# A selective state-space layer beside an MLP: the decay factors in PSUM, C turned on GpSimd, and another order at the end of a sequence's VectorE program

## The chip, the cores and the metric

The kernel runs on one core of one Trainium2 chip. The metric is the device time of one launch, in microseconds (us), that is from the first instruction to the last as the device reports it. A core has five engines with a queue of instructions each: TensorE (PE in the profile; its weight loads are PEld), VectorE (DVE), ScalarE (ACT), GpSimd (POOL), and SyncE (SP), whose queue issues the DMAs here. Every engine takes its own instructions strictly in order. What has to wait for another engine waits on a semaphore, and all that stands behind it in the same queue waits too.

## What is computed

Eight sequences of 512 tokens, 128 features wide. Each is normalised, and the result is the input plus a state-space branch plus an MLP branch. Cut to what matters:

```python
xn   = layernorm(x)                                   # (8, 512, 128)
z, xBC, dt = split(xn @ in_proj_w.T)                  # 256, 256+64+64, 4 heads
dt   = softplus(dt + dt_bias)
x_ssm, B, C = split(silu(causal_conv4(xBC)))
B_c, C_c = complex(B[0::2], B[1::2]), complex(C[0::2], C[1::2])   # 32 pairs
theta = clip(theta_base + tanh(xn @ w1) @ w2, -pi/2, pi/2)        # (4 heads, 32)
log_z = complex(-(lambda_base + eta * theta**2) * dt, theta * dt)
# chunks: S_t = exp(cumlog_t) * S_0 + sum_{s<=t} exp(cumlog_t - cumlog_s) * B_s * (x_ssm*dt)_s
y    = real(C_c . S) + D * x_ssm
g    = rmsnorm(y * silu(z)) * norm_w
attn = g @ out_proj_w.T
mlp  = s2 * relu2(s1 * relu2(s0 * [xn, -xn] @ K0) @ K1) @ K2      # K of +1 and -1, 128-512-512-128
out  = x + attn + mlp
```

The decay of a pair (s, t) is split into a factor of s and a factor of t, so that a product of matrices does the sum: with phase p and summed log decay c, K = exp(-c) (cos p, sin p) on the side of s, Q = exp(c) C (cos p, sin p) on the side of t, and U = Q times B for the part that needs B at the side of t.

## The kernel before

State data is laid out as 128 partitions (4 heads of 32 pairs) by 512 tokens, so most operations of VectorE, ScalarE and GpSimd are one instruction on a tile of 128x512 numbers of 4 bytes. The eight sequences are software-pipelined by hand: each engine has a function `pipelined(n, ...)` that writes out its order for the front of sequence n (projections, phases, decays, MLP), the back of sequence n-1 (G products, states, y, gate, output projection) and the start of sequence n+1 (layernorm, its transposes, the projection of dt, x, B and C). A loop of three rounds runs two sequences each; sequences 0, 7 and the last back stand outside it. There is no scheduler: the order of the code is the order of the queues, and a class `Signal` counts the steps of each stage on a semaphore. `s_kq` counts the steps of `decayed`, `s_u` those of `u_products`, `s_dt` the small steps of dt, `s_mo` the sum of the MLP (`add_mlp`), `s_bk` those of `b_and_k`.

The pieces that the change touches, by engine:

- VectorE, `dt_input` and `dt_steps`: softplus of dt as a chain of tiny instructions on 128x16 numbers, each waiting for the one ahead. All tiles lie in SBUF.
- VectorE, `exponents`: the log decay `lz` (L580), its running sum (L586), and the sum clipped (L587), after which ScalarE takes exp(-c) into `E` and exp(c) into `E2` (`decays`).
- VectorE, `decayed`: part 0 makes Kre and Kim (L603, L604). Part 1 makes `ec`, `es` (L608, L609). Parts 2 and 3 turn C by the phase (L613 to L615, three instructions each) into Qre and Qim.
- GpSimd: `b_and_k` (B times the conjugate of K, six instructions) and then `u_products` (Q times B, six instructions, L1141 to L1144), which waits for all of `decayed`.
- TensorE: the order around the seam between two sequences is `mlp1` (L1310, L1311), `x_products(n + 1, 0)` (L1262), `mlp_out` (L1319), `bc_products(n + 1)` (L1273), `lora1` of the next sequence (L1248), then the G products of the back, L1329, which wait for `s_mo`, `s_dt` and `s_u`, and `g_across` (L1339), which waits for `s_bk`.
- VectorE's tail of a sequence: `h1_low` 2 and 3 (L723, which release `mlp_out`), `x_times_dt` (L539), `dt_steps` of the next sequence, `add_mlp` (L727), `largest` (L651).

## Time and profile before

| What | us |
|---|---|
| Median of 3 runs | 410.99 (410.89 to 411.18) |
| The profiled execution, its own time | 410.37 |
| Its span (first to last instruction) | 407.0 |
| From one sequence's first G product to the next one's, in the middle | 44.3 |

The profiled execution lies 0.6 us under the median, and 3.4 us of its time lie outside the span. A busy time of an engine is the sum of its instructions. The chain of waits is followed back from the last instruction: each step is what released the one behind it. In a timeline row a bracket tells how long the engine stood idle ahead of the instruction, and who ended that. The mean granted TensorE clock of the execution was 0.941 of full speed.

### The profile page before, as it was taken

To read this page: it belongs to the slowest core of one execution; us is meant where nothing else is said; L and a number is where in the kernel's file an instruction comes from. 1 tells how busy PE (TensorE), PEld (TensorE's weight loads), DVE (VectorE), ACT (ScalarE), POOL (GpSimd) and SP (SyncE) were. 2 spreads that over 40 slices of the span, in tenths; PEclk is the share of its full clock that TensorE was granted. 3 is DMA by queue.
4 is the path that set the end of the run, shared out by engine and by line. 5 is a ranking of instruction groups with operands and counts; after the bars stand their busy time and mean duration, and the time that the engine had idled before them with its cause. 6 is when DMAs were issued, how large, how long until landed. Compare 5 with 4: busy or idle time off the path is not lost.

```text
span 407.0 us, 9993 instructions
## 1 busy us (share of the span) xinstructions
PE 334.8 (82%) x3962; PEld 234.9 (58%) x3962; DVE 310.3 (76%) x655; ACT 171.7 (42%) x305; POOL 147.6 (36%) x124
## 2 busy tenths in 40 slices
PE   0469289889979997989979997999799997895582
PEld 0444146577657664776567765766477655752571
DVE  2695789688968897789958896889868994888221
ACT  0307643375317714473427531771447343651020
POOL 1001077107621465107810762136610880076301
PEclk9999579999989999999989998999989998998896
DMA  7101200320023001400031002300040003000001
GB/s 192 15 0 40 64 0 2 81 52 2 27 61 73 2 0 42 108 14 0 27 84 48 2 27 62 73 2 2 26 122 11 0 27 85 23 2 26 2 2 31
DMA packets 19097, 14.86 MB, mean 36 GB/s; under 512 B 5045, under 2 KB 14826, under 8 KB 19050
## 3 DMA queue, kind: packets, MB, share of 16 engines
q1 hardware_dynamic: 16090, 13.67, 12.8%
q10 hardware_dynamic: 2960, 0.49, 0.7%
q8 instruction: 37, 0.61, 0.6%
q14 instruction: 10, 0.08, 0.1%
HBM read 3.67 MB, written 2.10 MB: 14 GB/s over the span
## 4 chain that ended last, share of the span: by engine, by line
DVE 47%; PE 26%; issue 11%; ACT 10%; POOL 2%; DMA 2%; SPq 1%; DVEq 1%; ACTq 0%; POOLq 0%
PE bank L1329 6%; PE bank L1420 4%; DVE h1l L723 3%; PE bank L1397 3%; DVE tmpd L614 3%; PE bank L1281 2%; DVE xd L539 2%; DVE phl L554 2%; DVE tmpc L613 2%; PE bank L1339 2%; DVE cum L586 2%; DVE ds L521 2%; DVE dacc L525 2%; DVE osb L736 2%; ACT z L970 2%
## 5 line engine op out<-in xcount | busy, mean ns | idle before, releaser
L1310 PE MATMUL bank<-h0h,W 128*128 128x512 f16 x128 | 50.3, 393 | 4.7 <-DVE h1l L723 3.2
L1160 POOL TENSOR_TENSOR btmp<-Kre,bres 128x512 f32<-128x512 f32 x8 | 8.5, 1059 | 125.5 <-DVE Kim L604 125.5
L1311 PE MATMUL bank<-h0l,W 128*128 128x512 f16 x128 | 50.1, 392 | 0.0
L1262 PE MATMUL bank<-XW,xh 128*128 128x256 f16 x256 | 49.1, 280 | 0.0
L1113 POOL TENSOR_TENSOR rstd<-vare,minus_half 128x4 f32<-128x4 f32 x8 | 8.1, 1018 | 77.0 <-DVE negmean L501 77.0
L1262 PE MATMUL bank<-XW,xl 128*128 128x256 f16 x128 | 35.7, 279 | 0.0
L1329 PE MATMUL bank<-Ure,Kre 32*128 32x128 f32 x256 | 20.3, 395 | 17.1 <-DVE o L727 12.8
L658 DVE TENSOR_TENSOR GT<-bank,const 128x512 f32<-128x512 f32 x32 | 19.9, 683 | 14.0 <-PE bank L1339 13.9
L1262 PEld LDWEIGHTS bank<-XW,xh 128*128 128x128 f16 x256 | 25.5, 100 | 7.1 <-issue 0.4
L938 ACT ACTIVATE de<-dneg 128x16 f32<-128x16 f32 x8 | 1.7, 216 | 65.2 <-DVE dneg L514 65.2
L1329 PEld LDWEIGHTS bank<-Ure,Kre 32*128 32x128 f32 x256 | 16.2, 287 | 20.6 <-issue 18.1
L1018 ACT ACTIVATE h1h<-bank 128x512 f16<-128x512 f32 x32 | 18.2, 591 | 21.7 <-PE bank L1311 21.7
L970 ACT ACTIVATE z<-bank 128x512 f32<-128x512 f32 x16 | 8.7, 594 | 43.7 <-PE bank L1281 43.7
L723 DVE SCALAR_TENSOR_TENSOR h0l<-bank,h0h 128x512 f16<-128x512 f32 x32 | 20.7, 687 | 7.1 <-ACT h0h L1018 7.1
L495 DVE BATCH_NORM_STATS2 st<-xtok 128x6 f32<-128x128 f32 x32 | 7.0, 280 | 23.9 <-DMA xtok<-in_x 19.1
L1310 PEld LDWEIGHTS bank<-h0h,W 128*128 128x128 f16 x128 | 12.8, 100 | 21.5 <-DVE h1l L723 4.9
L1420 PE MATMUL bank<-OW,gT 128*128 128x128 f32 x128 | 16.4, 281 | 7.4 <-DVE gT L715 7.4
L723 DVE SCALAR_TENSOR_TENSOR h1l<-bank,h1h 128x512 f16<-128x512 f32 x32 | 21.3, 681 | 1.4 <-ACT h1h L1018 1.1
L1361 PE MATMUL bank<-GT,xd 128*64 128x128 f32 x256 | 20.3, 279 | 0.5 <-issue 0.4
L1311 PEld LDWEIGHTS bank<-h0l,W 128*128 128x128 f16 x128 | 12.8, 100 | 13.4 <-issue 1.5
L1420 PEld LDWEIGHTS bank<-OW,gT 128*128 128x128 f32 x128 | 14.9, 191 | 9.5 <-DVE gT L715 9.5
L1273 PE MATMUL bank<-xh,BCW 128*128 128x512 f16 x64 | 20.4, 379 | 0.0
(193 smaller groups left out, 989.6 us busy)
## 6 DMA issues: line engine op xcount, KB each, us to landing
xtok<-in_x SPq DMA_DIRECT2D x8, 256.0 KB, 3.1
cres<-bc SPq DMA_DIRECT2D x32, 64.0 KB, 2.2
cims<-bc SPq DMA_DIRECT2D x32, 64.0 KB, 2.3
bres<-bc SPq DMA_DIRECT2D x32, 64.0 KB, 2.1
bims<-bc SPq DMA_DIRECT2D x32, 64.0 KB, 2.1
out<-osb SPq DMA_DIRECT2D x8, 256.0 KB, 2.3
const<-constants SPq DMA_DIRECT2D x1, 576.0 KB, 5.6
KT<-in_in_proj_w SPq DMA_DIRECT2D x1, 320.0 KB
```

Of the source, the lines that this page charges most:

```text
L614: step(V.tensor_tensor(t2, second[0], second[1], ALU.mult))
L658: V.tensor_tensor(GT[:, h, :, :], gbanks[fast][h][:].rearrange("p (c t) -> p c t", t=CH), view(const, 0, 128, mask, [[0, NCH], [1, CH]]), ...
L723: V.scalar_tensor_tensor(lo[:, f, :], bank[4 + f % 2][:], 0.0, high[:, f, :], ALU.max, ALU.subtract).then_inc(sig.sem, 1)
L970: step(a_silu, A.activation(z2s[p][:, half, :], bank[6 + half][:], ACT.Silu, scale=1 / PS))
L1018: step(sig, A.activation(hi[:, f, :], bank[4 + f % 2][:], ACT.Relu))
L1262: last = M.matmul(dst, tok(x, c, k), w[:, k, :], start=False, stop=(k == TAPS - 1 and q == 2))
L1273: last = M.matmul(bank[2][:], w[:, k, :], x[:, k:k + T], start=(k == 0 and q == 0), stop=(k == TAPS - 1 and q == 2))
L1310: M.matmul(bank[4 + f % 2][:], w, h0h[:, k, :], start=(k == 0), stop=False)
L1311: last = M.matmul(bank[4 + f % 2][:], w, h0l[:, k, :], start=False, stop=(k == MT - 1))
L1329: last = M.matmul(banks[h][:, width * c:width * c + width], view(left[0], 32 * h, 32, left[1] + CH * c, [[1, CH]]), rhs, start=(r == 0), s ...
L1361: last = M.matmul(y_part(h, CH * c, CH), xd[:, c, HEAD * h:HEAD * h + HEAD], GT[:, h, c, :], start=(c == 0), stop=True, skip_group_check=True)
L1420: last = M.matmul(out_in[:, D * c:D * c + D], gT[:, h, CH * c:CH * c + CH], OW[:, h, :], start=(h == 0), stop=(h == 1))
```

## The change

Four things, in one edit:

1. PSUM in place of SBUF. `lz` becomes TensorE's bank 2 (written in place over what the product is made of), both exponentials go to one tile `growth`, which is bank 3 (exp(-c) first, and exp(c) over it once K is made), and most of dt's small tiles go to columns of bank 1. So that each instruction has at most one input in SBUF, dt's chain has 13 instructions where it had 12, and its input 3 where it had 2.
2. GpSimd turns C: `c_rotated` makes R = C (cos p, sin p) without the decay, as soon as sine and cosine are there, and `b_times_rotated` makes B times R. VectorE's `decayed` is left with three pairs of multiplications by `growth`: K, Q = R growth, U = (B R) growth in place. U is so finished by VectorE and no longer by GpSimd.
3. VectorE's order: `final` and `dt_input` stand earlier; `x_times_dt` and `dt_steps` stand ahead of `h1_low` 2; `decayed(n, 2)` between `h1_low` 2 and 3; `add_mlp` right behind `h1_low` 3.
4. Waits that follow: TensorE's `lora1` (it writes bank 3) and the G products wait for `s_kq`, the transposes of xn (bank 2) for the running sum, the G products (bank 1 is one of theirs) for all steps of dt; ScalarE's second exponential waits for Kre and Kim; the DMAs of B for the next sequence wait for `b_and_k`.

```diff
-        dt_in = bank[1][:, 288:288 + NCH * HEADS]
+        dt_in, dv, dneg, dsum, dq, dacc = (
+            bank[1][:, 288 + NCH * HEADS * k:288 + NCH * HEADS * (k + 1)].rearrange("p (c h) -> p c h", h=HEADS) for k in range(6))
+        lz, growth = bank[2], bank[3]
@@ repeat_bc
-                    sp.wait_ge(s_u.sem, s_u.at(n, 0))
+                    sp.wait_ge(s_bk.sem, s_bk.at(n, 0))
@@ dt_input
-                step(V.scalar_tensor_tensor(dv[:], ps, 1.0 / PS, bias, ALU.mult, ALU.add))
-                step(V.scalar_tensor_tensor(dneg[:], dv[:], -1.0, dv[:], ALU.mult, ALU.min), linked=False)
+                step(V.scalar_tensor_tensor(dv[:], dt_in, 1.0 / PS, bias, ALU.mult, ALU.add), linked=False)
+                step(V.scalar_tensor_tensor(dvs[:], dt_in, 1.0 / PS, bias, ALU.mult, ALU.add))
+                step(V.scalar_tensor_tensor(dneg[:], dv[:], -1.0, dvs[:], ALU.mult, ALU.min), linked=False)
@@ dt_steps
-                step(V.tensor_scalar(ds[:], de[:], 2.0, None, ALU.add))
-                step(V.reciprocal(dq[:], ds[:]))
-                step(V.tensor_tensor(ds[:], de[:], dq[:], ALU.mult))
-                step(V.tensor_tensor(dq[:], ds[:], ds[:], ALU.mult))
-                step(V.tensor_scalar(dacc[:], dq[:], ATANH[-1], None, ALU.mult))
+                step(V.tensor_scalar(dsum[:], de[:], 2.0, None, ALU.add))
+                step(V.reciprocal(dq[:], dsum[:]))
+                step(V.tensor_tensor(dr[:], de[:], dq[:], ALU.mult), linked=False)
+                step(V.tensor_tensor(dsum[:], de[:], dq[:], ALU.mult))
+                step(V.tensor_tensor(dr2[:], dr[:], dsum[:], ALU.mult))
+                step(V.tensor_scalar(dacc[:], dr2[:], ATANH[-1], None, ALU.mult))
...
@@ decayed
+                step.count[0] = 2 * part
+                if part == 0:
+                    v.wait_ge(a_trig.sem, a_trig.done(n))
+                    v.wait_ge(a_exp.sem, a_exp.at(n, 1))
+                elif part == 1:
+                    v.wait_ge(a_exp.sem, a_exp.at(n, 2))
+                    v.wait_ge(s_rot.sem, s_rot.done(n))
                 else:
-                    rotated(step, part, Qim[:], (cres[:], es[:]), (cims[:], ec[:]), ALU.add, True)
+                    v.wait_ge(s_v.sem, s_v.done(n))
+                for dst, src in (((Kre, pcs), (Kim, psn)), ((Qre, Rre[:]), (Qim, Rim[:])), ((Ure, Ure[:]), (Uim, Uim[:])))[part]:
+                    step(V.tensor_tensor(dst[:], src, growth[:], ALU.mult), linked=False)
@@ decays (ScalarE)
-                        step(a_exp, A.activation(E[:], cum3[:, 0, :], ACT.Exp, scale=-1.0))
+                        step(a_exp, A.activation(growth[:], cum3[:, 0, :], ACT.Exp, scale=-1.0))
...
-                step(a_exp, A.activation(E2[:], cum3[:, 0, :], ACT.Exp))
+                if fast:
+                    act.wait_ge(s_kq.sem, s_kq.at(n, 2))
+                step(a_exp, A.activation(growth[:] if fast else E2[:], cum3[:, 0, :], ACT.Exp))
@@ gpsimd
-            def u_products(n):
...
+            def turned(sig, n, re, im, left):
+
+                (a, b), (c, d) = left
+                for k, (dst, f1, f2, op) in enumerate(((re, c, d, ALU.subtract), (im, d, c, ALU.add))):
+                    P.tensor_tensor(btmp[0][:], a[:], f1, ALU.mult).then_inc(sig.sem, 1)
+                    P.tensor_tensor(btmp[1][:], b[:], f2, ALU.mult).then_inc(sig.sem, 1)
+                    g.wait_ge(sig.sem, sig.at(n, 3 * k + 2))
+                    P.tensor_tensor(dst[:], btmp[0][:], btmp[1][:], op).then_inc(sig.sem, 1)
+                    g.wait_ge(sig.sem, sig.at(n, 3 * k + 3))
+
+            def c_rotated(n):
+                g.wait_ge(c_in.sem, c_in.done(n))
+                g.wait_ge(a_trig.sem, a_trig.done(n))
+                turned(s_rot, n, Rre, Rim, ((cres, cims), (pcs, psn)))
+
+            def b_times_rotated(n):
+                g.wait_ge(b_in.sem, b_in.done(n))
+                turned(s_v, n, Ure, Uim, ((bres, bims), (Rre[:], Rim[:])))
@@ xn_transposed (TensorE)
-                    pe.wait_ge(s_ph.sem, s_ph.at(n - 1, PHASE_STEPS + 1))
+                    pe.wait_ge(s_ph.sem, s_ph.at(n - 1, PHASE_STEPS + 2))
```

What that does to the queues is seen at three places.

GpSimd, one sequence in the loop before (`btmp` are its two scratch tiles; ISA and REGISTER_ALU rows are the sequencer's own):

```order
L1160 TENSOR_TENSOR btmp<-Kre,bres 128x512
L1161 TENSOR_TENSOR btmp<-Kim,bims 128x512
L1162 ISA
L1163 TENSOR_TENSOR Bre<-btmp 128x512
L1164 REGISTER_ALU
L1119 TENSOR_TENSOR rms<-msq,minus_half 128x4
L1160 TENSOR_TENSOR btmp<-Kim,bres 128x512
L1161 TENSOR_TENSOR btmp<-Kre,bims 128x512
L1162 REGISTER_ALU
L1163 TENSOR_TENSOR Bim<-btmp 128x512
```

The same place now, from the first product of C to `rms`; behind it stand the six instructions of B times R and then the six of B times K:

```order
L1145 TENSOR_TENSOR btmp<-cres,Xre 128x512
L1146 TENSOR_TENSOR btmp<-cims,Xim 128x512
L1147 ISA
L1148 TENSOR_TENSOR Rre<-btmp 128x512
L1149 REGISTER_ALU
L1145 TENSOR_TENSOR btmp<-cres,Xim 128x512
L1146 TENSOR_TENSOR btmp<-cims,Xre 128x512
L1147 REGISTER_ALU
L1148 TENSOR_TENSOR Rim<-btmp 128x512
L1149 REGISTER_ALU
L1126 TENSOR_TENSOR rms<-msq,minus_half 128x4
```

`rms` of the back stands behind the six instructions that turn C, B times K has moved from first to last, and a sequence has 18 large instructions on GpSimd where it had 12.

VectorE, the end of a sequence before (from `h1_low` 2 and 3 on; the rows between L525 and L530 are dt's):

```order
L723 SCALAR_TENSOR_TENSOR h1l<-bank,h1h 128x512 x2
L539 TENSOR_TENSOR xd<-x,dt 128x1024
L521 TENSOR_SCALAR ds<-de 128x16
L522 RECIPROCAL dq<-ds 128x16
L523 TENSOR_TENSOR ds<-de,dq 128x16
L524 TENSOR_TENSOR dq<-ds 128x16
L525 TENSOR_SCALAR dacc<-dq 128x16
L527 SCALAR_TENSOR_TENSOR dacc<-dacc,dq 128x16 x4
L528 SCALAR_TENSOR_TENSOR dacc<-dacc,ds 128x16
L529 TENSOR_SCALAR dv<-dv 128x16
L530 SCALAR_TENSOR_TENSOR dt<-dacc,dv 128x16
L727 SCALAR_TENSOR_TENSOR o<-bank,sffn,xtok 128x512
```

And now, from dt's last step on:

```order
L534 SCALAR_TENSOR_TENSOR dt<-bank,dmax 128x16
L728 SCALAR_TENSOR_TENSOR h1l<-bank,h1h 128x512
L634 TENSOR_TENSOR Ure<-Ure,bank 128x512
L634 TENSOR_TENSOR Uim<-Uim,bank 128x512
L728 SCALAR_TENSOR_TENSOR h1l<-bank,h1h 128x512
L732 SCALAR_TENSOR_TENSOR o<-bank,sffn,xtok 128x512
```

The sum of the MLP (L727, now L732) stands right behind the `h1_low` that releases its product; x times dt and dt's chain have gone ahead of `h1_low` 2, and the two multiplications of U stand between `h1_low` 2 and 3.

TensorE, the seam between two sequences, before (with the semaphores each row waits for):

```order
L1248 MATMUL bank<-xh,TW 48x512 [waits theta_unclipped]
L1248 MATMUL bank<-xl,TW 48x512
L1248 MATMUL bank<-xh,TW 48x512
L1434 ISA [waits final,mlp_added]
L1435 ISA [waits dt_steps]
L1329 MATMUL bank<-Ure,Kre 128x128 [waits U_products]
```

And now (`decayed` is what VectorE's last multiplication of U counts):

```order
L1263 MATMUL bank<-xh,TW 48x512 [waits decayed]
L1263 MATMUL bank<-xl,TW 48x512
L1263 MATMUL bank<-xh,TW 48x512
L1449 ISA [waits final,mlp_added]
L1450 REGISTER_ALU [waits dt_steps]
L1344 MATMUL bank<-Ure,Kre 128x128 [waits decayed]
```

The order of the products is the same; what they wait for comes from VectorE alone.

## Rows read from the trace of the kernel before

**Rows 1.** The page: busy time of each engine, and the chain by engine.

```profile
PE 334.8 (82%) x3962; PEld 234.9 (58%) x3962; DVE 310.3 (76%) x655; ACT 171.7 (42%) x305; POOL 147.6 (36%) x124
DVE 47%; PE 26%; issue 11%; ACT 10%; POOL 2%; DMA 2%; SPq 1%; DVEq 1%; ACTq 0%; POOLq 0%
```

**Rows 2.** Waits: who waited for whom, us in total, times, longest.

```profile
PE bank L1329 <- DVE o L727: 12.8, 7, 2.3
```

**Rows 3.** Timeline of TensorE, sequence 4: start, us, instruction, idle before and releaser.

```profile
205.56 0.71 PE L1329 MATMUL bank<-Ure,Kre 32*128 32x128 f32 x8 [2.25 <-DVE o L727]
...
209.18 0.34 PE L1339 MATMUL bank<-Qre,Bre 32*64 32x64 f32 x8
...
227.96 0.39 PE L1310 MATMUL bank<-h0h,W 128*128 128x512 f16 x1
...
242.20 0.23 PE L1319 MATMUL bank<-W,h1h 128*128 128x128 f16 x1 [0.36 <-DVE h1l L723]
...
247.56 0.39 PE L1248 MATMUL bank<-xh,TW 128*48 128x512 f16 x1 [0.81 <-issue]
...
249.86 0.64 PE L1329 MATMUL bank<-Ure,Kre 32*128 32x128 f32 x8 [1.47 <-DVE o L727]
```

**Rows 4.** Timeline of TensorE at the first seam, from sequence 0 to sequence 1.

```profile
67.64 0.22 PE L1319 MATMUL bank<-W,h1h 128*128 128x128 f16 x1
...
69.43 0.38 PE L1273 MATMUL bank<-xh,BCW 128*128 128x512 f16 x1
...
74.22 0.50 PE L1329 MATMUL bank<-Ure,Kre 32*128 32x128 f32 x8 [1.27 <-DVE o L727]
...
76.22 0.34 PE L1339 MATMUL bank<-Qre,Bre 32*64 32x64 f32 x8
```

**Rows 5.** Windows of 1 us: length, busy PE, PEld, DVE, ACT, POOL, granted clock, DMA.

```profile
75.00:76.00 1.00, 1.00 (x45) 1.00 (x40) 0.00 (x0) 0.00 (x0) 0.00 (x0) 1.00 0.68 205
207.00:208.00 1.00, 1.00 (x28) 1.00 (x27) 0.00 (x0) 0.00 (x0) 0.00 (x0) 0.50 0.88 281
```

**Rows 6.** Timeline of VectorE, the same sequence 4.

```profile
213.56 0.43 DVE L546 TENSOR_SCALAR theta<-tin 128x512 f32<-128x512 f32 x1 [0.63 <-ACT tin L974]
...
222.25 0.43 DVE L587 TENSOR_SCALAR cum<-cum 128x512 f32<-128x512 f32 x1
...
225.67 0.68 DVE L604 TENSOR_TENSOR Kim<-Xim,E 128x512 f32<-128x512 f32 x1
...
229.47 0.94 DVE L608 TENSOR_TENSOR ec<-Xre,E 128x512 f32<-128x512 f32 x1 [0.90 <-ACT sq L1005]
...
242.06 1.46 DVE L539 TENSOR_TENSOR xd<-x,dt 128x1024 f32<-128x1024 f32 x1
243.45 1.23 DVE L521 TENSOR_SCALAR ds<-de 128x16 f32<-128x16 f32 x1
...
248.79 0.75 DVE L727 SCALAR_TENSOR_TENSOR o<-bank,sffn,xtok 128x512 f32<-128x512 f32 x1
```

**Rows 7.** Timeline of GpSimd, the same sequence.

```profile
229.94 1.35 POOL L1119 TENSOR_TENSOR rms<-msq,minus_half 128x4 f32<-128x4 f32 x1
...
238.61 1.27 POOL L1141 TENSOR_TENSOR btmp<-Qre,bres 128x512 f32<-128x512 f32 x1 [3.15 <-DVE Qim L615]
...
242.52 2.13 POOL L1141 TENSOR_TENSOR btmp<-Qim,bres 128x512 f32<-128x512 f32 x1
```

**Rows 8.** Timeline of ScalarE, the same sequence: the cosine.

```profile
219.59 0.71 ACT L988 ACTIVATE Xre<-pabs,halfpi 128x512 f32<-128x512 f32 x1
```

**Rows 9.** VectorE, groups by form: busy us, mean ns of one, idle before.

```profile
L614 DVE TENSOR_TENSOR tmpd<-cims,es 128x512 f32<-128x512 f32 x8 | 12.5, 1567 | 0.0
...
L723 DVE SCALAR_TENSOR_TENSOR h1l<-bank,h1h 128x512 f16<-128x512 f32 x32 | 21.3, 681 | 1.4 <-ACT h1h L1018 1.1
```

**Rows 10.** Timeline of TensorE in sequence 7, the last front.

```profile
360.32 0.39 PE L1310 MATMUL bank<-h0h,W 128*128 128x512 f16 x1
...
379.88 0.81 PE L1329 MATMUL bank<-Ure,Kre 32*128 32x128 f32 x8 [4.29 <-POOL Uim L1144]
```

More of the change, by code:

```diff
@@ L532, in wait_past @@
+                step(V.scalar_tensor_tensor(dacc[:], dacc[:], 1.0, dr[:], ALU.add, ALU.mult), linked=False)
+                step(V.tensor_scalar(dmax[:], dv[:], 0.0, None, ALU.max))
+                step(V.scalar_tensor_tensor(dt[:], dacc[:], 2.0, dmax[:], ALU.mult, ALU.add))
             def wait_past(sig, n):
@@ L780, in pipelined @@
                     h1_low(n, 0)
-                    decayed(n, 2)
-                    h1_low(n, 1)
-                    decayed(n, 3)
-                if next_loaded is not None:
-                    dt_input(n + 1)
                 if has_back:
@@ L788, in pipelined @@
                 if has_front:
-                    h1_low(n, 2)
-                    h1_low(n, 3)
+                    h1_low(n, 1)
+                if next_loaded is not None:
+                    dt_input(n + 1)
+                if has_front:
                     x_times_dt(n, p)
@@ L794, in pipelined @@
                 if has_front:
+                    h1_low(n, 2)
+                    decayed(n, 2)
+                    h1_low(n, 3)
                     add_mlp(n, p)
@@ L1240, in dt_products, with lora1 @@
                     for k, (x, w) in enumerate(pairs(DTW)):
-                        last = M.matmul(dt_in[:, HEADS * c:HEADS * c + HEADS], tok(x, c), w[:], start=(k == 0), stop=(k == 2))
+                        last = M.matmul(dt_in[:, c, :], tok(x, c), w[:], start=(k == 0), stop=(k == 2))
                 last.then_inc(t_dt.sem, 1)
-            def lora1(n):
+            def lora1(n, fast):
                 if not (isinstance(n, int) and n == 0):
                     pe.wait_ge(a_th.sem, a_th.at(n, 0))
+                    pe.wait_ge(s_kq.sem, s_kq.at(n, 0) if fast else s_kq.done(SEQS - 1))
                 for k, (x, w) in enumerate(pairs(TW1)):
```

64 lines of the change are left out of this document (22 added, 42 removed).

## The prediction, made before the changed kernel ran

> **What bounds the kernel now.** I read the page first, then the waits, then one middle sequence on each engine, because the loop repeats it. TensorE is busy for 334.8 of 407.0 us and VectorE for 310.3, and the chain that ends last runs 47% over VectorE and 26% over TensorE [rows 1]: neither bounds alone, they hand the end to each other. The place is the seam between two sequences. TensorE's longest wait in total is that of the first G product for the MLP sum (`add_mlp`, L727): 12.8 us in 7 times [rows 2]. In sequence 4 it is 1.47 us, and with it goes a gap of 0.36 us ahead of `mlp_out` and one of 0.81 us at the loop's branch [rows 3]. From `mlp1` (227.96) to 241.84 TensorE has no gap. The product that `add_mlp` waits for is done near 244.0, but VectorE reaches `add_mlp` only at 248.79, since x times dt (from 242.06) and dt's 12 small steps (from 243.45) stand ahead of it [rows 6].
>
> There is a second price at this seam. The 64 small G products take 3.62 us in sequence 4 (205.56 to 209.18) [rows 3] and 2.00 us at the first seam (74.22 to 76.22) [rows 4]. In the first case the granted clock is 0.50 (1.2 GHz), in the second 1.00 (2.4 GHz) [rows 5]. What TensorE did before differs: it had stood idle for 2.25 us, against 1.27 us at the first seam. A shorter idle time there also gives back 1.6 us of clock.
>
> **The change part by part, in the times of sequence 4.**
>
> *PSUM inputs.* A multiplication of two SBUF tiles takes VectorE 1.57 us on average while GpSimd works (`tmpd`), but `Kim`, alone, takes 0.68, and `h1l`, which reads a bank and one SBUF tile, takes 0.68 in all company [rows 6, 9]. So K, Q and U by `growth` cost 0.6 to 0.7 us each, whatever GpSimd does. VectorE spent from 229.47 to 238.53 on the eight instructions that make Q and on two `h1_low` (238.61 less GpSimd's start lag) [rows 6, 7]; now two multiplications, 1.3 us. That VectorE reads a bank written by itself (`lz`) as fast as one of TensorE's is taken from `h1l`; no row shows it.
>
> The Trainium skill says why ("SBUF — State Buffer", Who interferes with whom): with at most one SBUF input, outside its two-port modes, a VectorE instruction doesn't meet GpSimd at all. The rows of `h1l` agree.
>
> *C turned on GpSimd.* An instruction on two full tiles takes it 1.27 us; with the waits ahead of the subtractions six of them take 7.8 us [rows 7]. It can start when the cosine is done, 219.59 + 0.71 = 220.30 [rows 8]. VectorE's clipping of the sum (L587, ready at 222.25) has its input and output in SBUF and now meets it: like dt's first step at 243.45, 1.23 us long for 16 numbers, it waits until GpSimd's instruction ends. GpSimd's second ends near 222.9, so L587 ends 0.5 us later. The bounds are 0 (it falls between two) and 1.2 (it meets a fresh one); I take 0.5. This lies on the path, because `gated` half 1, `out_products` and the copies of `h0` hang on it: `mlp1` starts 0.5 later. A rule of the skill speaks against this part ("Perfetto Trace Analysis", Optimizing Scalar/DVE Operations): since GpSimd and VectorE share a read port, moving work between the two might not help. If VectorE's remaining multiplications still met GpSimd at `tmpd`'s price the six would cost 5 us more; by the row of `h1l` they don't.
>
> GpSimd then runs: C turned, 220.4 to 228.6 (7.8 plus 0.4 while L587 holds it up); `rms` for the back, held until the mean squares at about 229.1, to 230.4 (1.35) [rows 7]; B times R, 7.8, plus 1.1 behind x times dt (it waited as long at 242.52: 2.13 for 1.27), to 239.4; B times K, six at 1.27 or less, to 247 at most. Q waits for the first (228.6), where VectorE comes at about 229.2: no wait. U waits for the third.
>
> *VectorE's new order.* Q to 230.5, `h1_low` 0 (its copy comes from `mlp1`) to 231.8, `final` to 232.8, `h1_low` 1 to 233.5, dt's input to 234.1, x times dt behind one GpSimd instruction to 235.4, 13 steps of dt, 2.7, to 238.1 (the 12 took 5.3 us from 243.45 to 248.79, three of them held about 1 us each by GpSimd, which leaves 0.2 for one). `h1_low` 2 to 238.8, then U at 239.5 to 240.8, `h1_low` 3 to 241.5. TensorE ends `x_products` at 241.8 + 0.5 = 242.3. So `mlp_out` waits no more, with 0.8 us to spare. Behind it VectorE has nothing but `add_mlp`, 0.75 us, ready 0.8 us behind `mlp_out` while TensorE has B, C and `lora1` to do. If that cover is gone (U late by more than 0.8), each us is a us of the seam. Two tensor_scalar steps of dt read SBUF and write PSUM, of which there is no row: at worst each waits for a GpSimd instruction, 2 x 1.2, at best nothing. I take nothing, since their inputs lie next to `h1l`'s case; the worst leaves U late by 1.6.
>
> *What the moved waits do.* The transposes of xn wait for the running sum, 1.2 us longer, but behind them TensorE waited for the gate anyway. The second exponential waits for K, made before it comes up. `lora1` waits for U: 1.5 us and more before it. The G products' wait for all of dt: done at 238. The next x is loaded once `add_mlp` is done, now some 3 us ahead of the G products, so layernorm is no longer late behind the DMA. B's DMAs wait for B times K, at about the old time. `g_across` needs B times K (247) at about 249.5. All these at nothing.
>
> *The sum for a sequence*, from G product to G product: 8.0 to theta (213.56 - 205.56) less 1.6 for the clock, 6.4; theta to `mlp1`, 14.4 + 0.5; `mlp1` to the end of `x_products`, 13.9; `mlp_out`, B and C and `lora1` without a gap, 67.64 to 72.95 at the first seam [rows 4], 5.3; 0.1 to start. That is 40.6, and 41.5 where the loop branches back (0.9, of which two show). Before it was 44.3 (249.86 - 205.56) in the middle and 43.1 behind the first seam. Six such stretches: five at 44.1 on average and one at 43.1, so 263.6, become 4 x 40.6 + 2 x 41.5 = 245.4: 18.2 saved. Sequence 0: the gap of 1.27 at the first seam goes, less 0.35 for L587: 0.9. Sequence 7: its clock 1.3 (its seam was half fast), less 0.5; then from `mlp1` (360.32) to the G products (379.88), 19.6 us, ended by GpSimd's last product, 4.29 of wait [rows 10]. Now U is done 12.3 after `mlp1`, `mlp_out` and `add_mlp` follow by 15.6, or 17.3 if the clock falls in the wait, and B times K ends at 18.2, which `g_across` needs 2 to 3.7 behind the start: 2.9 saved, from 1.6 to 4. In all 18.2 + 0.9 + 0.8 + 2.9 = 22.8. From the profiled execution's own 410.37 that leaves 387.6, and 0.6 more against the median: **388**.
>
> **The rivals.**
>
> *The clock falls all the same (388 + 10 = 398).* The idle time may not be what decides, or the gap at the branch may be enough for 0.50. Then 1.6 us return at six seams. For it: sequences 2 to 7 all had it. Against it: at the first seam 1.27 us of idle time did not bring it down, and now 0.1 to 0.9 are left.
>
> *U comes late (394).* Both steps of dt meet GpSimd, or GpSimd runs a little slower in its longer company: U late by 1.6, less nothing of spare, 0.9 to 1.6 at six seams, 5 to 10 us; 394 in the middle. The rows for steps of one SBUF input and PSUM output are missing, so I can't exclude it.
>
> *GpSimd bounds and the kernel is slower (about 420).* Place: B times R ahead of U, 12 large instructions from the cosine to U, with VectorE's `h1_low` 3 and `add_mlp` queued behind the wait for U, and TensorE behind them. The gain of a sequence is about 3.3; 0.8 are spare; with an idle time of TensorE the clock's 1.6 return too. So it decides from 2.5 us later, 0.2 us on each of 12: a mean of 1.5 us in place of 1.27. At 1.65, 4.6 late, less 0.8, plus 1.6, less 3.3: 2.1 slower by seven sequences, and with sequence 0, 425 at most, 420 with some overlap. For it: instructions of GpSimd that meet VectorE took up to 2.13 us [rows 7]. Against it: they did so where VectorE worked on two SBUF tiles, and only L587, x times dt and `largest` are left of those.
>
> *It does not do what it says (411).* `add_mlp` still ends late for a reason that no row shows, such as VectorE's own reads of its PSUM tiles, and the gain in VectorE's queue only becomes idle time.
>
> **How the numbers follow.** TensorE-bound seams at the full clock 0.63, the clock falling 0.12, U late 0.14, slower by GpSimd 0.05, no effect 0.02, and 0.04 for more gain than I count (the end of sequence 7 at 4, L587 at 0, and starts without a gap: 381). The likeliest case runs from 384 to 391 by its own bounds. To hold 8 in 10 the range takes in the clock and U late: 381 to 398. A measurement can tell 0.2% from no change, 0.8 us: faster 0.93, the same 0.02, slower 0.05.
>
> **What would show it.** `Kre` to `Uim` at 0.6 to 0.7 us each; GpSimd from the cosine on without a gap but at `rms`, its instructions at 1.27; L587 at 0.9 to 1.0; no wait of TensorE for `add_mlp`; 2.0 us from the first G product to `g_across` at a granted clock of 1.00; 40.6 us from seam to seam. I am wrong if TensorE waits at `mlp_out` for `h1_low` 3 behind U, if the clock at the G products reads 0.50, or if L587 costs more than 1.2.

## The result, and the profile after

The changed kernel takes 385.44 us, the median of four runs (382.23 to 390.05), beside 410.94 (410.82 to 411.18) for the kernel before: a ratio of 0.935 with a 95% interval of 0.928 to 0.943. The ratio leaves out the run of 390.05, which counts as a slow one. The forecast was 388. The profiled execution took 387.12 us, of which 384.9 are its span.

The page of the kernel after, the busy times and the chain, to be laid beside [rows 1]:

```profile
PE 327.5 (85%) x3962; PEld 229.6 (60%) x3962; DVE 254.2 (66%) x639; ACT 173.2 (45%) x305; POOL 199.5 (52%) x172
PE 65%; DVE 20%; ACT 4%; issue 4%; POOL 3%; DMA 2%; SPq 1%; DVEq 0%; POOLq 0%
```

VectorE has lost 56 us of work and GpSimd has gained 52. The chain went 47% over VectorE; now it goes 65% over TensorE. TensorE's own work is the same; it reads 7 us less because it ran at the full clock more of the time.

Waits of the kernel after (who waited for whom, us in total, times, longest), to be laid beside [rows 2]:

```profile
DVE o L732 <- PE bank L1334: 27.5, 8, 3.7
...
PE bank L1435 <- DVE gT L720: 9.3, 8, 1.8
...
PE bank L1334 <- DVE h1l L728: 4.9, 1, 4.9
...
PE bank L1344 <- DVE o L732: 0.8, 1, 0.8
```

The wait of [rows 2] has turned round: TensorE waited 12.8 us in seven seams for the sum of the MLP; now it waits once, in sequence 7, and the sum waits some 3.4 us for TensorE in every sequence. Sequence 4 on TensorE, for [rows 3]:

```profile
195.66 0.50 PE L1344 MATMUL bank<-Ure,Kre 32*128 32x128 f32 x8
...
197.66 0.34 PE L1354 MATMUL bank<-Qre,Bre 32*64 32x64 f32 x8
...
212.41 2.05 PE L1435 MATMUL bank<-OW,gT 128*128 128x128 f32 x16 [1.08 <-DVE gT L720]
...
216.91 0.39 PE L1325 MATMUL bank<-h0h,W 128*128 128x512 f16 x1
...
230.62 0.22 PE L1334 MATMUL bank<-W,h1h 128*128 128x128 f16 x1
...
235.87 0.39 PE L1263 MATMUL bank<-xh,TW 128*48 128x512 f16 x1 [0.70 <-issue]
...
236.62 0.50 PE L1344 MATMUL bank<-Ure,Kre 32*128 32x128 f32 x8
```

From seam to seam it is 40.96 us (236.62 - 195.66), where it was 44.30. No row at the seam has a wait but the branch's, and the G products take 2.00 us in place of 3.62. Windows of 1 us, for [rows 5] (length, busy PE, PEld, DVE, ACT, POOL, granted clock, DMA), one in these G products and one in the last MLP product of sequence 7:

```profile
196.00:197.00 1.00, 1.00 (x46) 1.00 (x41) 0.89 (x5) 0.87 (x2) 0.00 (x0) 1.00 0.06 14
...
352.00:353.00 1.00, 1.00 (x12) 1.00 (x10) 0.00 (x0) 0.00 (x0) 0.92 (x2) 0.50 0.00 0
```

VectorE in the same sequence, for [rows 6]:

```profile
210.73 0.90 DVE L591 TENSOR_SCALAR cum<-cum 128x512 f32<-128x512 f32 x1
...
214.61 0.68 DVE L634 TENSOR_TENSOR Kim<-Xim,bank 128x512 f32<-128x512 f32 x1
...
222.19 1.38 DVE L543 TENSOR_TENSOR xd<-x,dt 128x1024 f32<-128x1024 f32 x1
223.50 0.17 DVE L524 TENSOR_SCALAR bank<-de 128x16 f32<-128x16 f32 x1
...
225.87 0.18 DVE L534 SCALAR_TENSOR_TENSOR dt<-bank,dmax 128x16 f32<-128x16 f32 x1
...
227.31 0.69 DVE L634 TENSOR_TENSOR Ure<-Ure,bank 128x512 f32<-128x512 f32 x1
...
228.51 0.68 DVE L728 SCALAR_TENSOR_TENSOR h1l<-bank,h1h 128x512 f16<-128x512 f32 x1
...
232.61 0.75 DVE L732 SCALAR_TENSOR_TENSOR o<-bank,sffn,xtok 128x512 f32<-128x512 f32 x1 [3.41 <-PE bank L1334]
```

And GpSimd, for [rows 7]: `rms`, the one instruction of B times R that meets x times dt, and the last of B times R.

```profile
217.66 1.02 POOL L1126 TENSOR_TENSOR rms<-msq,minus_half 128x4 f32<-128x4 f32 x1 [0.97 <-DVE msq L724]
...
222.57 2.13 POOL L1145 TENSOR_TENSOR btmp<-bres,Rim 128x512 f32<-128x512 f32 x1
...
226.01 1.27 POOL L1148 TENSOR_TENSOR Uim<-btmp 128x512 f32<-128x512 f32 x1
```

Sequence 7, for [rows 10], on VectorE and TensorE:

```profile
348.86 0.69 DVE L634 TENSOR_TENSOR Ure<-Ure,bank 128x512 f32<-128x512 f32 x1 [3.11 <-POOL Uim L1148]
```

```profile
350.80 0.29 PE L1334 MATMUL bank<-W,h1h 128*128 128x128 f16 x1 [4.94 <-DVE h1l L728]
...
355.24 0.81 PE L1344 MATMUL bank<-Ure,Kre 32*128 32x128 f32 x8 [0.84 <-DVE o L732]
```

There is no next sequence's work here to fill the time, so U waits for GpSimd, the last `h1_low` stands behind U, and TensorE is idle for 4.94 us. What follows runs at a granted clock of 0.50 (the second window above), until 359.8.

### The profile page after: what moved, and what is told of

It reads as the page before. It is cut to its first block, busy times and chain, and to the rows that moved or that the text cites. A ratio compares the mean times of both kernels' runs of the same rounds, so it can differ in the third digit from the quotient of the medians.

```text
span 384.9 us, 9989 instructions
## 1 busy us (share of the span) xinstructions
PE 327.5 (85%) x3962; PEld 229.6 (60%) x3962; DVE 254.2 (66%) x639; ACT 173.2 (45%) x305; POOL 199.5 (52%) x172
## 4 chain that ended last, share of the span: by engine, by line
PE 65%; DVE 20%; ACT 4%; issue 4%; POOL 3%; DMA 2%; SPq 1%; DVEq 0%; POOLq 0%
PE bank L1277 12%; PE bank L1325 7%; PE bank L1326 6%; PE bank L1288 5%; PE bank L1344 5%; PE bank L1435 4%; PE bank L1334 4%; PE bank L1427 3%; PE bank L1412 3%; PE bank L1296 3%; DVE phl L558 3%; DVE cum L590 3%; PE bank L1354 2%; ACT z L975 2%; DVE cum L591 2%
## 5 line engine op out<-in xcount | busy, mean ns | idle before, releaser
L1145 POOL TENSOR_TENSOR btmp<-cres,Xre 128x512 f32<-128x512 f32 x8 | 10.2, 1272 | 84.8 <-ACT Xre L993 84.8
L1325 PE MATMUL bank<-h0h,W 128*128 128x512 f16 x128 | 49.4, 386 | 1.4 <-DVE h0l L728 1.4
L1326 PE MATMUL bank<-h0l,W 128*128 128x512 f16 x128 | 49.3, 385 | 0.0
L1025 ACT ACTIVATE h1h<-bank 128x512 f16<-128x512 f32 x32 | 19.1, 597 | 48.0 <-PE bank L1326 48.0
L663 DVE TENSOR_TENSOR GT<-bank,const 128x512 f32<-128x512 f32 x32 | 19.9, 683 | 19.4 <-PE bank L1354 19.4
L732 DVE SCALAR_TENSOR_TENSOR o<-bank,sffn,xtok 128x512 f32<-128x512 f32 x8 | 6.0, 750 | 27.5 <-PE bank L1334 27.5
L1126 POOL TENSOR_TENSOR rms<-msq,minus_half 128x4 f32<-128x4 f32 x8 | 8.2, 1020 | 27.7 <-DVE msq L724 27.7
L1325 PEld LDWEIGHTS bank<-h0h,W 128*128 128x128 f16 x128 | 12.7, 99 | 16.5 <-DVE h0l L728 2.3
L1435 PEld LDWEIGHTS bank<-OW,gT 128*128 128x128 f32 x128 | 14.9, 191 | 11.5 <-DVE gT L720 11.5
L1376 PE MATMUL bank<-GT,xd 128*64 128x128 f32 x256 | 21.2, 288 | 0.4 <-issue 0.4
L1334 PE MATMUL bank<-W,h1h 128*128 128x128 f16 x128 | 16.7, 231 | 4.9 <-DVE h1l L728 4.9
L1326 PEld LDWEIGHTS bank<-h0l,W 128*128 128x128 f16 x128 | 12.7, 99 | 13.7 <-issue 0.8
L1383 PE MATMUL bank<-skip_eye,x 128*64 128x128 f32 x256 | 20.4, 282 | 0.0
L1025 ACT ACTIVATE h0h<-bank 128x512 f16<-128x512 f32 x32 | 17.3, 589 | 6.4 <-PE bank L1316 6.4
```

What stands on the lines that cost most here:

```text
L663: V.tensor_tensor(GT[:, h, :, :], gbanks[fast][h][:].rearrange("p (c t) -> p c t", t=CH), view(const, 0, 128, mask, [[0, NCH], [1, CH]]), ...
L1025: step(sig, A.activation(hi[:, f, :], bank[4 + f % 2][:], ACT.Relu))
L1325: M.matmul(bank[4 + f % 2][:], w, h0h[:, k, :], start=(k == 0), stop=False)
L1326: last = M.matmul(bank[4 + f % 2][:], w, h0l[:, k, :], start=False, stop=(k == MT - 1))
L1334: last = M.matmul(bank[4][:, D * c:D * c + D], h[:, k, CH * c:CH * c + CH], W2[:, k, :], start=(k == 0 and r == 0), stop=(k == MT - 1 and ...
L1376: last = M.matmul(y_part(h, CH * c, CH), xd[:, c, HEAD * h:HEAD * h + HEAD], GT[:, h, c, :], start=(c == 0), stop=True, skip_group_check=True)
```

## The experiments

Theory at the start: the seam became TensorE's because all of the edit together, the PSUM inputs, C on GpSimd and the new order, brought VectorE to the sum of the MLP early enough. First rival: one part does it, and the others shift work that was hidden. Second rival: the gain is mostly the clock. All ratios below are to the kernel before, run in the same company.

### dt's tiles in PSUM, alone

The kernel before with only the tiles of dt moved to bank 1 (3 and 13 steps), its order and GpSimd's work left as they were:

```diff
-        dt_in = bank[1][:, 288:288 + NCH * HEADS]
+        dt_in, dv, dneg, dsum, dq, dacc = (
+            bank[1][:, 288 + NCH * HEADS * k:288 + NCH * HEADS * (k + 1)].rearrange("p (c h) -> p c h", h=HEADS) for k in range(6))
...
```

> The kernel before with one part of the change alone: dt's small tiles in bank 1 (13 steps, inputs 3), and the G products' wait for all of them. C is turned on VectorE and U made on GpSimd as before, the order as before. My theory, read again from both traces: the seam is paid by what stands ahead of the MLP sum on VectorE, and of that 2.9 us are dt's steps held up by GpSimd; the shorter idle time then brings the clock back too. Without the 2.9 us the MLP sum is done about 3 us earlier, U on GpSimd (247.3 against 249.9 for the G product) ends last, so 2.5 us plus 1.6 of clock at six seams: about 386 us, as fast as the whole change. Rival (the whole change is needed, since C's turn holds VectorE as well): dt alone gives at most its 2.9 us less what U allows, at a clock that stays at 0.50: 396 or above.

Measured: 387.52 us (385.96 to 389.37), ratio 0.948 (0.943 to 0.952). The end of VectorE's sequence in it, at the same place of the program:

```profile
229.29 2.26 DVE L540 TENSOR_TENSOR xd<-x,dt 128x1024 f32<-128x1024 f32 x1
231.47 0.16 DVE L521 TENSOR_SCALAR bank<-de 128x16 f32<-128x16 f32 x1
...
234.05 0.75 DVE L728 SCALAR_TENSOR_TENSOR o<-bank,sffn,xtok 128x512 f32<-128x512 f32 x1
```

In the kernel before, two more steps of dt had stood behind GpSimd, besides the first one [rows 6]:

```profile
245.00 0.91 DVE L523 TENSOR_TENSOR ds<-de,dq 128x16 f32<-128x16 f32 x1
...
246.16 1.13 DVE L525 TENSOR_SCALAR dacc<-dq 128x16 f32<-128x16 f32 x1
```

dt's chain takes 2.6 us (231.47 to 234.05) where it took 5.3, the sum is done at 234.8, and TensorE begins its G products at 235.74 with no wait, at the full clock. A sequence takes 40.1 to 41.1 us, as in the whole change. U from GpSimd now comes last at four other seams, by 0.2 to 0.4 us, and the clock stays up behind these waits. So the theory put down for this run, about 386, holds, and with it the first rival of the whole change: moving tiles of 16 numbers per partition carries most of the gain, and perhaps all.

### The whole change without dt's tiles in PSUM

```diff
-        dt_in, dv, dneg, dsum, dq, dacc = (
-            bank[1][:, 288 + NCH * HEADS * k:288 + NCH * HEADS * (k + 1)].rearrange("p (c h) -> p c h", h=HEADS) for k in range(6))
+        dt_in = bank[1][:, 288:288 + NCH * HEADS].rearrange("p (c h) -> p c h", h=HEADS)
+        dv, dneg, dsum, dq, dacc = (sb(f"dts{k}", [128, NCH, HEADS])[:] for k in range(5))
```

> The changed kernel with dt's small tiles back in SBUF, all else as changed. Four or five of the small steps read two SBUF tiles, or one in the two-port mode, and wait for GpSimd, which now works without a pause there: dt's part 3 to 4 us longer on VectorE, ahead of h1_low 2, U and h1_low 3. These have about 2 us to spare in the trace (h1_low 3 done 229.2, x products done 230.6): mlp_out 1 to 2 us later in each of seven sequences, clock partly down: 393 to 403 us. If it stays at 385 to 387, dt's tiles in PSUM are worth nothing here.

Measured: 434.0 us (432.7 to 435.1), ratio 1.059 (1.056 to 1.062). Slower than the kernel before, and 49 us over the change where I had put down 8 to 18. dt's chain on VectorE, and TensorE's longest wait:

```profile
251.88 1.23 DVE L524 TENSOR_SCALAR dts<-de 128x16 f32<-128x16 f32 x1
...
253.44 0.90 DVE L526 TENSOR_TENSOR dr<-de,dts 128x16 f32<-128x16 f32 x1
...
254.46 1.23 DVE L528 TENSOR_TENSOR dr<-dr,dts 128x16 f32<-128x16 f32 x1
...
255.93 3.30 DVE L531 SCALAR_TENSOR_TENSOR dts<-dts,dr 128x16 f32<-128x16 f32 x4
```

```profile
PE bank L1334 <- DVE h1l L728: 38.5, 8, 4.9
```

A step of 0.17 us takes up to 1.23: it waits until GpSimd's instruction ends. In the kernel before three of the twelve did, and then GpSimd's run was over (at 247.25, in the times of [rows 7]). Here GpSimd works on until 262.7 with hardly a gap: eight of the thirteen steps wait, some of the others slip in between two of GpSimd's instructions (0.16 to 0.17 us), and the chain takes 9.5 us (251.88 to 261.4). My 393 to 403 counted four or five meetings. On TensorE the wait for `h1_low` grows from 4.9 to 38.5 us, and the same instructions are busy for 343.4 us in place of 327.5, at a lower mean clock (0.902 in place of 0.954): together that is the whole loss. The price goes by the number of instructions and by how gapless GpSimd is, not by how much data they move. 434 is this change's dangerous side: without dt in PSUM the rest costs 24 us.

### The decay factors back in SBUF

```diff
-        lz, growth = bank[2], bank[3]
+        lz, growth = bank[2], E
```

> The changed kernel with the two exponentials of the decay in an SBUF tile in place of bank 3 (dt's tiles and the log decay stay in PSUM). Only the six multiplications of K, Q and U then read two SBUF tiles. Theory: next to GpSimd each takes the 1.57 us that such instructions took in the kernel before, 0.9 more than 0.68, so VectorE is 5.4 us later at the second half of h1; 1.4 of it are spare there, 4.0 become an idle time of TensorE ahead of the MLP's last product in seven sequences, 28 us, and with it the clock falls at six seams, 10 us: about 413 to 423. Rival (the decay factors in PSUM buy little, it is dt's tiles that matter): under 392.

Measured: 395.6 us (392.96 to 397.99), ratio 0.964 (0.956 to 0.971): 10 us over the change, or 7 if the change is taken at 388.6, as it was measured again later. I had put down 413 to 423, its rival under 392: with C on GpSimd the part is worth something, but a third of what I thought. The log decay stayed in PSUM, and what that is worth was not tried. The multiplications, grouped by name (busy us in all, mean ns):

```profile
L634 DVE TENSOR_TENSOR Kim<-Xim,E 128x512 f32<-128x512 f32 x8 | 14.0, 1755 | 0.0
...
L634 DVE TENSOR_TENSOR Uim<-Uim,E 128x512 f32<-128x512 f32 x8 | 12.8, 1598 | 0.0
L634 DVE TENSOR_TENSOR Qre<-Rre,E 128x512 f32<-128x512 f32 x8 | 6.5, 815 | 0.8 <-POOL Rim L1148 0.8
```

Two of the six meet GpSimd, not all: `Kre` and `Ure` start in the gap before GpSimd's next instruction, and Q comes while GpSimd waits for `rms`. So 2 us a sequence on VectorE and not 5.4, but they stand on the path to `h0_low` (TensorE waits 5.6 us for it in seven times, 1.4 before in one) and to `h1_low` 3. GpSimd waits too: its busy time grows from 199.5 to 216.2 us, another 2 us a sequence that the forecast didn't have, and U comes later by it.

### C turned by VectorE again

The six multiplications and sums of C back on VectorE, with everything in PSUM as changed and the last `h1_low` ahead of U:

```diff
...
                 if has_front:
-                    decayed(n, 1)
+                    turn_c(n, 0)
                     h1_low(n, 0)
-                if has_back:
-                    final(n - 1, pq, stored)
-                if has_front:
+                    turn_c(n, 1)
+                    decayed(n, 1)
                     h1_low(n, 1)
+                if has_back:
+                    final(n - 1, pq, stored)
@@ gpsimd
                 if has_front:
-                    c_rotated(n)
+                    b_and_k(n, s_kq, 0)
                 if has_back:
                     rms_of(n - 1)
                 if has_front:
-                    b_times_rotated(n)
-                    b_and_k(n, s_kq, 0)
                     b_and_k(n, s_kq, 1)
+                    b_times_rotated(n)
...
```

> The changed kernel, with the last h1_low ahead of U, but C turned by VectorE again (six multiplications and sums of two SBUF tiles, without the decay) and GpSimd back to twelve large instructions, B times K first. Everything that the change put into PSUM stays there. Theory (dt's tiles are what carried the gain, turning C on GpSimd only shifts work that has room on either engine): VectorE gets some 4 to 9 us more a sequence, R is ready near 226 in the times of sequence 4, B times R on GpSimd ends near 234 and the sum of the MLP near 236.4, just where the G products begin (236.6): 385 to 391. Rival (C on GpSimd is needed): U comes several us late in every sequence, TensorE waits for the sum at the seam and the clock falls: 400 and more.

Measured: 407.2 us (405.6 to 408.4), ratio 0.994 (0.991 to 0.997). My theory fell here. TensorE and VectorE in sequence 4 of this kernel:

```profile
222.61 2.05 PE L1448 MATMUL bank<-OW,gT 128*128 128x128 f32 x16 [0.60 <-DVE gT L732]
...
237.57 0.39 PE L1338 MATMUL bank<-h0h,W 128*128 128x512 f16 x1 [1.57 <-DVE h1l L740]
...
244.52 0.23 PE L1347 MATMUL bank<-W,h1h 128*128 128x128 f16 x1 [1.79 <-DVE h1l L740]
```

```profile
221.41 0.43 DVE L591 TENSOR_SCALAR cum<-cum 128x512 f32<-128x512 f32 x1
```

It isn't U that comes late, as the rival had it: TensorE waits for the `h1_low` halves (14.2 us in eight times inside `mlp1`, and 1.8 in each of six sequences ahead of `mlp_out`). VectorE has 7.4 us more, some 3 of them waits behind GpSimd, and this run puts nearly all of it ahead of `h1_low` 1: that is the wait inside `mlp1`. Behind it x times dt with dt's chain, 4.3 us, stands ahead of `h1_low` 2 and 3, where in the kernel with dt alone it stands behind them: that is the wait ahead of `mlp_out`. So this order of VectorE has no room for C. That C has to go to GpSimd isn't shown: the kernel with dt alone turns C on VectorE in the old order and takes 387.5. C on VectorE with the old order and the decay factors in PSUM was not tried.

The same run prices one term: with GpSimd idle there, L591 takes 0.43 us and the output products wait 0.60; with C on GpSimd 0.90 and 1.08. So L591 costs 0.47 us on the path in sequence 4, as the forecast's 0.5 had it.

### The order at the end undone

```diff
-                    x_times_dt(n, p)
-                    dt_steps(n + 1)
                     h1_low(n, 2)
                     decayed(n, 2)
                     h1_low(n, 3)
+                    x_times_dt(n, p)
+                    dt_steps(n + 1)
                     add_mlp(n, p)
```

> The changed kernel with VectorE's tail back in the old order: h1_low 2, U, h1_low 3, then x times dt, dt's steps, and only then the MLP sum. With dt's steps at 2.5 us they end near the end of the MLP product, and B, C and lora1 (3.4 us on TensorE) cover the rest: no more than 0.3% slower than the change, 384 to 388 us. Rival (the title's last part, the MLP sum right behind its product, carries the gain): the wait for the MLP sum returns, 1 us and the clock, over 395.

Measured: 383.92 us (383.03 to 385.87), ratio 0.939 (0.936 to 0.943), the same as the change. With C on GpSimd and dt cheap there is room on VectorE for either order.

### How near GpSimd is

Two more full instructions on GpSimd ahead of B times R:

```diff
+                for k in range(2):
+                    P.tensor_tensor(btmp[0][:], Rre[:], Rim[:], ALU.mult).then_inc(s_more.sem, 1)
+                    g.wait_ge(s_more.sem, s_more.at(n, k + 1))
```

> The changed kernel with two further instructions of full tiles on GpSimd (1.27 us each) ahead of B times R: how near GpSimd is to being the bound. In sequence 4 the last of B times R ended at 227.3, when VectorE reached U; h1_low 3 was done 1.4 us before TensorE needed it. Theory: U and h1_low 3 come 2.5 us later, TensorE waits 1.1 us ahead of the last MLP product in seven sequences and 2.5 in sequence 7, 10 us: 395, and up to 403 if the clock falls at some seams as it did with waits of 1.3 to 2.1 us. Rival (there is more room than it looks): within 2 us of 385.

Measured: 397.9 us (396.7 to 399.2), ratio 0.972 (0.965 to 0.978). In sequence 4, and in sequence 7, ahead of `mlp_out`:

```profile
236.77 0.23 PE L1338 MATMUL bank<-W,h1h 128*128 128x128 f16 x1 [1.27 <-DVE h1l L729]
...
362.83 0.29 PE L1338 MATMUL bank<-W,h1h 128*128 128x128 f16 x1 [7.73 <-DVE h1l L729]
```

2.5 us more of GpSimd become 1.27 us of wait in each of sequences 1 to 6, so 1.2 were spare. The forecast of 395, up to 403, holds. That is 0.1 us on each of the 12 instructions from the cosine to U. The run also answers the rival of a slower kernel. Its place was right, but its price was too high: GpSimd 2.5 us later was to use up the whole gain, with 1.6 us of clock among it, and the run is still 3% faster than the kernel before. TensorE waits ahead of `mlp_out` and not at the seam, and the G products stay at 2.00 us in all eight.

### Idle time and the clock

Six, then eight idle instructions of VectorE ahead of the sum of the MLP, to hold the G products back:

```diff
                 v.wait_ge(t_mo.sem, t_mo.done(n))
+                for _ in range(6):
+                    step(V.scalar_tensor_tensor(tmpa[:], bank[5][:], 0.0, h1h[:, 3, :], ALU.max, ALU.subtract))
```

> The changed kernel with six idle VectorE instructions of 0.68 us between the end of the MLP product and the sum of the MLP, so that VectorE holds the G products back. In sequence 4 the sum ended at 233.4 and the G products began at 236.6; six linked instructions of some 0.74 us move the sum's end to about 237.8, so TensorE stands idle for about 1.2 us at each seam. Theory (the length of the idle time decides whether the clock falls, and 1.27 us at one seam before the change did not bring it down): the 64 G products still take 2.0 us at a granted clock of 1.00, a sequence takes 1.2 us more, sequence 7, where the sum is on the path, 4.4 more: about 397. Rival (any wait at this place brings the clock down): G products 3.6 us at 0.50 and 1.6 us more per sequence, about 407.

> The same with eight idle instructions: TensorE stands idle for about 2.6 us at each seam. Theory: the clock falls to its lower level at every seam, the G products take 3.6 us, a sequence is 2.6 + 1.6 us longer, and sequence 7 about 5.9: about 417. Rival (the clock is brought down by something else than this idle time): only 2.6 per sequence, G products 2.0 us, about 407.

Measured: 410.0 us (408.3 to 412.3), ratio 1.000 (0.996 to 1.004), and 427.8 (426.8 to 428.7), ratio 1.043 (1.036 to 1.050). With six, TensorE waited 1.32 to 2.11 us at the seven seams of sequences 0 to 6. The two seams at the loop's branch, each with the gap of the branch, the start of the G products and the first product behind them:

```profile
161.08 0.39 PE L1267 MATMUL bank<-xh,TW 128*48 128x512 f16 x1 [0.72 <-issue]
...
163.22 0.67 PE L1348 MATMUL bank<-Ure,Kre 32*128 32x128 f32 x8 [1.32 <-DVE o L736]
...
166.82 0.34 PE L1358 MATMUL bank<-Qre,Bre 32*64 32x64 f32 x8
...
248.89 0.39 PE L1267 MATMUL bank<-xh,TW 128*48 128x512 f16 x1 [0.65 <-issue]
...
251.11 0.50 PE L1348 MATMUL bank<-Ure,Kre 32*128 32x128 f32 x8 [1.39 <-DVE o L736]
...
253.10 0.34 PE L1358 MATMUL bank<-Qre,Bre 32*64 32x64 f32 x8
```

Behind nearly the same idle time, 0.72 and 1.32 us the first time and 0.65 and 1.39 the second, the products took 3.60 us and 1.99. At the five other seams there is no such gap, and the wait is 1.84 to 2.11 us. In all, four of the seven seams ran slower (2.6, 3.6, 3.2, 3.0 us) and three at 2.0. With eight, the waits were 2.63 to 3.57 us and all seven slower (3.2 to 3.7). In the kernel with two more instructions on GpSimd the wait of 1.27 us lay 5 to 6 us ahead of the seam, and no seam was slow. In its sequence 7, with 7.73 us of idle time ahead of `mlp_out`, the clock read 0.50 from 359.7 to 366.6 and was back at 1.00 when the G products began at 367.3. So the longer the idle time right at the seam, the surer the fall, but its length alone doesn't decide it between 1.3 and 2.1 us.

For six instructions neither the theory (2.0 us for the products everywhere) nor its rival (3.6) came true; for eight the theory's lower clock did. Both runs are dearer than I had put down, by some 13 and 11 us. With six, TensorE's waits for the sum come to 17.9 us where 13.6 were forecast (1.2 at each of seven seams and 5.2 in sequence 7): the 1.2 was read at a seam of the branch, and without the branch's gap the wait is 2.0. The clock, put at nothing, makes TensorE's own instructions 7.6 us longer (335.1 us busy in place of 327.5). With 0.8 us of such waits in the changed kernel that makes 24.7 of the 25.1 us by which the span is longer. With eight the waits are 29.3 us, and the busy time is 12.4 us longer. The load of the next x, which waits for the sum, comes late too (VectorE waited 18.2 us for it, 13.1 in the changed kernel). But the kernel with the order at the end undone has 17.9 us of that wait and takes 383.9, so no price of it is shown.

### Three tries for a faster version

The last `h1_low` ahead of U, for sequence 7; the second half of the gate ahead of the clipping (L591), for the 1.08 us of the output products; and both.

```diff
                     h1_low(n, 2)
-                    decayed(n, 2)
                     h1_low(n, 3)
+                    decayed(n, 2)
                     add_mlp(n, p)
```

```diff
-                    step(V.tensor_tensor_scan(cum3[:, 1, :], all_ones(T), lz[:], 0.0, ALU.mult, ALU.add))
+                    step(V.tensor_tensor_scan(cum3[:, 1, :], all_ones(T), lz[:], 0.0, ALU.mult, ALU.add), linked=False)
+                    if between:
+                        between(4)
+                    step.link()
...
```

> The changed kernel with the last h1_low ahead of the two multiplications of U. In the loop VectorE is early enough for either order, so nothing changes there. In sequence 7 U waits for GpSimd until 348.9 and the last h1_low, done only at 350.7, kept TensorE idle for 4.94 us: now the MLP's product starts near 345.8 at the full clock, and the G products follow U and the sum at about 351.3 in place of 355.2. Theory: 3.5 to 5 us less than the changed kernel's 385.4, about 381. Rival (the end is set by something else, such as B times K on GpSimd, done at 355.8): within 1 us of 385.

> The changed kernel with the second half of the gate (gT, from bank 7) ahead of the clipping of the decay sum on VectorE. In the changed kernel the clipping (L591) stands 0.9 us long in GpSimd's way and the gate, which reads PSUM, stands behind it; TensorE waits 1.08 us for the gate there. In the other order the gate's 0.6 us fit into the clipping's wait: out_products start 1.0 us earlier, mlp1 0.8 earlier (then bound by h0_low 0). Seven sequences: 5 us less, about 380. Rival: the clipping itself sets mlp1 by way of exp, h0h and h0_low, and nothing is won: within 1 us of the change.

> Two small moves together, as a try for a faster version: the second half of the gate ahead of the clipping (a sequence 0.5 us shorter where the clock stays up) and the last h1_low ahead of U (in sequence 7 the G products 3.5 us earlier, of which GpSimd's B times K gives 2.9 back). By the rows of the two single runs: 385.4 less 3 less 1, about 381.5; if the clock falls at other places in their stead, as it did for the first of the two, 384 to 385.

> The changed kernel once more, in the same company as the other three, so that they can be compared with it directly: 382 to 390, as before.

(`between(4)` is the gate's second half.) Measured: 384.8 us (384.5 to 385.2), ratio 0.938 (0.933 to 0.943); 385.1 (382.6 to 386.0), ratio 0.939 (0.935 to 0.942); and both 384.2 (382.4 to 386.7), ratio 0.939 (0.932 to 0.947). The changed kernel again, beside the last: 388.6 (386.2 to 390.0), ratio 0.949 (0.943 to 0.956). So of the first two forecasts, about 381 and about 380, the rivals came true (within 1 us of the change), and both moves together are at the upper forecast of 384 to 385. The intervals of the last two overlap: no version that beats the change is shown. In the first, the G products of sequence 7 start 3.5 us earlier, and GpSimd gives most of it back:

```profile
351.74 0.50 PE L1344 MATMUL bank<-Ure,Kre 32*128 32x128 f32 x8 [1.64 <-DVE o L732]
356.74 0.34 PE L1354 MATMUL bank<-Qre,Bre 32*64 32x64 f32 x8 [2.94 <-POOL Bim L1176]
```

In the second, the output products' wait goes, and where the clock stays up a sequence is about 0.5 us shorter (39.9 in place of 40.4), but TensorE then waits 0.25 us for `h0_low`, and in its profile the clock fell twice behind the mean squares, once with 0.25 us of idle time shortly before and once with 0.59 and 0.38, at a price of 1.7 us each. Moves of half a microsecond drown in where the clock falls.

## Why the prediction held, step by step

**The seam.** Right. The wait for `add_mlp` is gone in seven sequences, G products at 2.00 us in all seven. Six stretches take 243.9 us (317.47 - 73.57) where 245.4 were forecast: 40.2 to 40.7 in the middle (forecast 40.6), 41.0 and 41.4 at the branch (41.5). The steps agree: G product to theta 6.4 (forecast 6.4), theta to `mlp1` 14.9 (14.9), `mlp1` to the end of `x_products` 13.7 (13.9).

**The durations.** K, Q and U take 0.68 us on average each; no meeting with GpSimd. The two steps of dt for which no row stood, with one SBUF input and a PSUM output, take 0.17 and 0.18 us: "nothing" was right, and the rival of a late U with it. L591 costs 0.47 on the path (0.5). The scan that reads `lz` from a bank takes 1.21. `rms` was put at 1.35 and took 1.02, with 0.97 of wait ahead. That layernorm would no longer be late behind the load of x was wrong: VectorE still waited 13.1 us for it in six sequences, but nobody waited for VectorE there. `h1_low` 3 was done at 229.2, where TensorE came at 230.6: 1.4 us spare and not 0.8; the run on GpSimd's nearness has 1.2.

**Where the gain comes from.** This is what the prediction doesn't say and the runs do. It told the new order as the reason why VectorE reaches `add_mlp` early. Taking the order at the end back out of the change costs nothing (383.9 without it), and dt's tiles alone give 387.5. The step that carries the sum is that dt's chain takes 2.6 us in place of 5.3, since three of its steps no longer wait for GpSimd. The seam lay close enough that 2.7 us less ended the wait, and with the wait went the clock's 1.6. The second rival, that the gain is mostly the clock, has a good third of it: the G products of the seven seams of sequences 0 to 6 took 22.6 us in all and take 14.0, and the waits ahead of them were 12.8. The other parts free VectorE (293.1 us busy with dt alone, 254.2 in the change), which nobody waited for after that. And they take away room: with GpSimd gapless, leaving dt in SBUF costs 49 us.

**Sequence 7 and the end.** The sum for it was 0.8 + 2.9; its stretch shrank by 4.1 us (from 41.89 to 37.77). The wait at `mlp_out` behind U stood in the working (U done 12.3 us behind `mlp1`; 11.4 measured) with the lower clock as the worse case, and that case came: the G products start 16.5 us behind `mlp1`, between the 15.6 and the 17.3. What is missing is the lower clock behind it. While TensorE still has work the granted clock is 0.50 until 359.8 and again from 363.2 to 366.6, where in the kernel before it was 0.50 once, until 383.2, and from the G products to the end of the span it takes 29.7 us in place of 27.1. In the kernel with the order at the end undone the clock was back before the G products of sequence 7, and the same stretch took 25.7. That is 2.5 us lost at a place to which I had given nothing.

**The account.** First seam 0.65 (forecast 0.9), six stretches 19.9 (18.2), sequence 7 4.1 (3.7), the end -2.5 (0), outside the span 1.1 (0): 23.2 us, which is 410.37 - 387.12. The forecast had 22.8. It came out right with two terms off in opposite directions, +1.7 and -2.5, and one that I had not looked at, so that the sum is this close is in part luck. The profiled execution also lies 1.7 us over the median of the changed kernel: against that, 385.4, the 388 is 2.6 too high.

**The rivals.** The clock falling all the same: no, seven seams at 2.00 us. But the reason given, that 1.27 us didn't bring it down once, is weaker than it looked. The trace of the kernel before has a seam with a shorter wait and the lower clock, 3.58 us for the products:

```profile
159.37 0.39 PE L1248 MATMUL bank<-xh,TW 128*48 128x512 f16 x1 [1.07 <-issue]
...
161.40 0.81 PE L1329 MATMUL bank<-Ure,Kre 32*128 32x128 f32 x8 [1.21 <-DVE o L727]
...
164.98 0.34 PE L1339 MATMUL bank<-Qre,Bre 32*64 32x64 f32 x8
```

It lies at the branch, so 1.07 us of gap stand close ahead of the wait. The forecast was right because the wait is now nothing: the branch's gap alone, 0.7 and 1.04 us, didn't bring the clock down. U late: only in sequence 7. GpSimd as the bound: not in this kernel, but with 1.2 us of room; with 2.5 us more the run is at 397.9, where the rival's working has the whole gain gone.

## What to carry to other kernels

An instruction of VectorE with two SBUF inputs, or one of the other forms that met GpSimd here, waits until the GpSimd instruction in flight has ended, however small it is itself; so look first for chains of tiny steps beside GpSimd's long ones, and move their tiles to PSUM, before moving big work between engines. When work goes to GpSimd, count again what meets it, because filled gaps raise the price of what is left: dt's chain in SBUF took 5.3 us before and 9.5 beside the longer run. And where a bound seam is freed, try the parts alone: what stands in the diff beside the part that counts may be worth nothing and still use up the room.
